# First pipeline step reordered: convolutions, pad clears, an integer-weight load and a gather change places

## The chip, the cores and the metric
One core of one Trainium2 chip. The metric is the device time of the kernel in microseconds (us), as a median of several executions.

## The reference
Sixteen images of 32 channels and 32 x 32 pixels go through a dense block and then through a quantised block. The dense block, cut to what matters:

```python
x1 = relu(conv2d(x, w1, b1, 2, 2))                       # 3x3, dilation 2
x2 = relu(conv2d(cat(x, x1), w2, b2, 2, 2))
x3 = relu(conv2d(cat(x, x1, x2), w3, b3, 2, 2))
x4 = relu(conv2d(cat(x, x1, x2, x3), w4, b4, 2, 2))
fea = einsum('ij,bcjk,lk->bcil', H, relu(cat(x, x1, x2, x3, x4)), H)
out = conv2d(fea, w6, b6, 1, 1) + x
```

The quantised block takes `out`, quantises activations and the weights w1, w2, w3 of its own to 4 bits (one scale for each whole tensor, from its largest magnitude), and computes a 1x1 convolution, a depthwise 3x3 convolution and a 1x1 convolution, with relu between them and a residual at the end.

## The kernel before
The images go in eight pairs; u = 0, 1 is the image in its pair. The dense block is a software pipeline of nine steps (`steps`): in step s each engine does the convolutions of pair s and the transform of pair s - 1. Step 0 has no transform to do, and its code has special cases under `is_first(s)`; step 8 has no convolutions. Every engine has its own instruction list, written out by hand, and engines wait for one another on semaphores. Nothing reorders the work of an engine.

Features 0 to 3 (x, x1, x2, x3) lie in SBUF as `D[f][u]`, 128 partitions: two quarters are the image's own rows, two are copies of them shifted by rows (halos), which the DMA makes out of the own rows (`halos(s, f, u)`: two transfers, lines 219 and 222; for f = 2 and u = 0 the second one is issued by ScalarE, `halo_2`, line 348). A high and a low part are kept of every feature for precision; `own_ready[u]` says that both stand. `clear_pads(f)` writes the zero borders of D[f] with eight small memsets on VectorE.

TensorE's work of a pair goes by weight groups:

- `conv0` or `conv0_first` (group 0, from x: sums of x1 and x2), `conv0_on` (group 1, from x: sums of x3 and x4), nine matmuls each. Neither needs a halo from the DMA: x is loaded with its shifted copies.
- `conv1_alone` (group 2, from D[1], six matmuls of the cross terms of x2), `conv1` (group 3, from D[1]), `conv2` (group 4, from D[2]), `conv3` (group 5, from D[3]). Each waits for the halos of its feature.

Around them: ScalarE's `relu` (x1, x3) and `take_part` (x2, x4) read the sums, `high_2` writes the high part of x2; VectorE's `split` and `split_2` write the parts of a feature and raise `own_ready`; `add_first` and `add_second` (together `add_parts`) join the halves of the sums of x2 and x4, and the second raises `added[u]`. `gather_x` and `gather(s, f, u)` on SyncE's queue copy the features into `F` for the transform (one transfer of line 229, two of line 239).

The weights of the quantised block (`w_int`) are loaded by SyncE's line 273 into `w_raw`, the buffer of the convolution weights, once the sixth of the low parts of these is made (`w_ready` at NM = 6). VectorE's `weight_peaks` (lines 594 to 596) finds their largest magnitudes, TensorE's `turn_peaks` transposes them (line 774), VectorE's `top_weights` reduces them, TensorE's `spread_weights` copies the result to all partitions (line 779), and step 1 needs the scales.

SyncE's list of step 0, and the wait that heads each transfer, sets when the halos go: two loads of x for the next pair, halos(1, 0), halos(1, 1), gather_x(0), gather(1, 0), gather_x(1), gather(1, 1), w_int, halos(2, 0), halos(2, 1), gather(2, 0), gather(2, 1), gather(3, 0), halos(3, 0), halos(3, 1), gather(3, 1), xb.

Of the kernel before, what the change touches and what calls it, by code (L numbers as in the profile page):

```python
# [77 lines left out]
def dense_block(nc, block, semaphore, x_res, x_pads, x_mix, w_conv, bias, w_mix, h_cols, h_rows, b6, w_int, ident_in, keep):  # L78
# [7 lines left out]
    with ExitStack() as ctx:  # L86
# [97 lines left out]
        def is_first(s):  # L184
            return isinstance(s, int) and s == 0
# [22 lines left out]
        @block.sync  # L208
        def _(sp):
            def load_x(s, p):  # L210
                for u in range(2):
                    sp.dma_start(x_own[p][u][:].rearrange("c a n -> c (a n)"),
                                 x_pads[s * 2 + u]).then_inc(x_in[p][u], 16)

            def halos(s, f, u):
                sp.wait_ge(own_ready[u], s * 3 + f)

                flat = D[f][u][:].bitcast(F32).rearrange("p h a n -> p h (a n)")
                sp.dma_start(flat[HALO_M2:HALO_M2 + 32, :, HALO:DSZ],
                             flat[OWN_T2:OWN_T2 + 32, :, 0:DSZ - HALO]).then_inc(halo_in[f][u], 16)  # L220
                if (f, u) != (2, 0):
                    sp.dma_start(flat[HALO_P4:HALO_P4 + 32, :, 0:DSZ - HALO],
                                 flat[OWN_T:OWN_T + 32, :, HALO:DSZ]).then_inc(halo_in[f][u], 16)

            def gather_x(s, u):

                if not is_first(s):
                    sp.wait_ge(f_lo[u], s)
                sp.dma_start(F[u][0:32].rearrange("p h n -> p (h n)"), x_mix[s * 2 + u]).then_inc(f0_in[u], 16)

            def gather(s, f, u):

                if f == 2:
                    sp.wait_ge(added[u], s * 2 + 1)
                else:
                    sp.wait_ge(relu_done[u], s * 2 + (f + 1) // 2)
                done, landed = (part[u], f2_in[u]) if f == 2 else (r[u], f_in[u])
                for h in range(2):
                    sp.dma_start(F[u][32 * f:32 * f + 32, h],
                                 done[32 * h:32 * h + 32].rearrange("p a b l -> p (a b l)")).then_inc(landed, 16)  # L240

            sp.dma_start(x_own[0][0][:].rearrange("c a n -> c (a n)"), x_pads[0]).then_inc(x_in[0][0], 16)
            sp.dma_start(w_raw[:, 0, :], w_conv[:, 0, :]).then_inc(w_in[0], 16)
            sp.dma_start(x_own[0][1][:].rearrange("c a n -> c (a n)"), x_pads[1]).then_inc(x_in[0][1], 16)
            sp.dma_start(bias_sb[:], bias).then_inc(c_in, 16)
            for n in range(1, NM):
                sp.dma_start(w_raw[:, n, :], w_conv[:, n, :]).then_inc(w_in[n], 16)
            sp.dma_start(hc[:].rearrange("p d l -> p (d l)"), h_cols).then_inc(h_in, 16)
            sp.dma_start(hr[:], h_rows).then_inc(h_in, 16)
            sp.dma_start(mix_raw.rearrange("p k m -> p (k m)"), w_mix).then_inc(mix_in, 16)  # L250
            sp.dma_start(b6_sb[:], b6).then_inc(c_in, 16)
            sp.dma_start(ident[:], ident_in).then_inc(id_in, 16)

            def step(s, odd, batch):
                p = s - 1
                if is_last(s):
                    return
                if not no_next(s):
                    if not is_first(s):
                        for u in range(2):  # L260
                            sp.wait_ge(x_split[u], s)
                    load_x(s + 1, 1 - odd)
                if is_first(s):
                    for u in range(2):
                        halos(s, 1, u)
                for u in range(2):
                    gather_x(s, u)
                    gather(s, 1, u)
                    if not is_first(s):
                        halos(s, 1, u)  # L270
                if is_first(s):
                    sp.wait_ge(w_ready, NM)
                    sp.dma_start(w_raw[:].rearrange("p n m -> p (n m)")[:, 0:W2], w_int).then_inc(int_in, 16)
                halos(s, 2, 0)
                halos(s, 2, 1)
                gather(s, 2, 0)
                gather(s, 2, 1)
                gather(s, 3, 0)
                halos(s, 3, 0)
                halos(s, 3, 1)  # L280
                gather(s, 3, 1)
                sp.wait_ge(mx_done, p + GRANT)
                sp.dma_start(xb[odd][:].rearrange("p u n -> p (u n)"), x_res[s]).then_inc(xb_in[odd], 16)

            steps(sp, step)
# [180 lines left out]
        def _(dve):  # L466
# [202 lines left out]
            def step(s, odd, batch):  # L669
                p = s - 1  # L670

                before = 1 - odd, batch - odd
                if is_last(s):
                    turn_s1(p - 1, 1)
                    turn_back(p - 1, 0)
                    turn_back(p - 1, 1)
                    add_up(p - 1, 0, *before)
                    turn_s1(p, 0)
                    add_up(p - 1, 1, *before)
                    turn_back(p, 0)  # L680
                    add_up(p, 0, odd, batch)
                    largest(p - 1, *before)
                    turn_s1(p, 1)
                    largest_last(0)
                    turn_back(p, 1)
                    add_up(p, 1, odd, batch)
                    largest_last(1)
                    return
                if is_first(s):
                    dve.wait_ge(zeroed, 2)  # L690
                if not is_second(s):
                    split(s, 1, 0)
                    if has_finish(s):
                        turn_s1(p - 1, 1)
                    split(s, 1, 1)
                if is_first(s):
                    for n in range(3, NM):
                        low_w(n)
                    low_mix()
                    clear_pads(2)  # L700
                add_parts(s, 2, 0)
                if is_first(s):
                    clear_pads(3)
                    dve.wait_ge(zeroed, 6)
                add_first(s, 2, 1)
                split_2(s, 0)
                add_second(s, 2, 1)
                split_2(s, 1)
                if has_finish(s):
                    turn_back(p - 1, 0)  # L710
                    turn_back(p - 1, 1)
                if not no_next(s):
                    low_x(s + 1, 1 - odd, 0)
                    low_x(s + 1, 1 - odd, 1)
                if has_finish(s):
                    add_up(p - 1, 0, *before)
                if is_first(s):
                    weight_peaks()
                if is_second(s):
                    quantise_weights()  # L720
                split(s, 3, 0)
                split(s, 3, 1)
                if is_first(s):
                    top_weights()
                if is_second(s):
                    sum_weights()
                    dve.wait_ge(fields_zeroed, 1)
                if has_finish(s):
                    add_up(p - 1, 1, *before)
                    largest(p - 1, *before)  # L730
                    into_fields(*before)
                if is_first(s):
                    low_f(s, 0)
                    split(1, 1, 0)
                add_parts(s, 4, 0)
                if is_first(s):
                    weight_scales()
                else:
                    low_f(s, 0)
                add_parts(s, 4, 1)  # L740
                low_4(s, 0)
                low_f(s, 1)
                if is_first(s):
                    split(1, 1, 1)
                else:
                    turn_s1(p, 0)
                low_4(s, 1)
# [4 lines left out]
        def _(pe):  # L752
# [55 lines left out]
            def conv0_on(s, u):  # L808
                weights(s, 2)
                conv(s, u, 0, 1, 1, True).then_inc(x_used[u], 1)  # L810
# [94 lines left out]
            def step(s, odd, batch):  # L905
# [28 lines left out]
                if is_first(s):  # L934
                    conv0_first(0)
                    conv0_first(1)
                    conv0_on(0, 0)
                    conv1_alone(0, 0)
                    conv0_on(0, 1)
                    conv1_alone(0, 1)  # L940
                else:
                    if is_second(s):
# [20 lines left out]
                conv2(s, 0)  # L963
                conv2(s, 1)
                if is_first(s):
                    turn_peaks()
                    conv0(1, 0)
                    conv0(1, 1)
                    spread_weights()
                if dct:  # L970
# [524 lines left out]
```

## Time and profile before

| | us |
|---|---|
| median of 3 runs | 396.76 |
| lowest of them | 396.33 |
| highest of them | 2032.51 |
| the profiled execution | 397.4 |
| its span, first to last instruction | 395.6 |
| its mean granted TensorE clock | 0.987 |

The median is the kernel's time here; one of the three runs was disturbed. The profile is of a further execution of 397.4 us, of which the span of 395.6 us is what the views show; 1.8 us lie around it. All times of rows are microseconds from the start of the span. Step 0 on TensorE ends at about 37.5 us.

### The profile page before, as it was taken

How to read it: one execution, taken by the hardware profiler on the slowest of the kernel's cores; microseconds unless marked ns; L12 is line 12 of the kernel's file. 1: busy time of each engine (PE TensorE's matmuls, PEld its weight loads, DVE VectorE, ACT ScalarE, POOL GpSimd, SP SyncE). 2: the span in 40 equal slices, each digit the busy share in tenths (PEclk: the TensorE clock that was granted, in tenths of full speed). 3: DMA queues.
4: the chain of work that ended last, by engine and by line, in shares of the span. 5: the costliest groups of instructions: out<-in, count | busy, mean ns of one | idle time of the engine just before them, and what ended most of it. 6: DMA issues, size and time to landing. Idle time of an engine off the chain costs nothing.

```text
span 395.6 us, 8022 instructions
## 1 busy us (share of the span) xinstructions
PE 372.0 (94%) x2873; PEld 270.7 (68%) x2873; DVE 289.1 (73%) x545; ACT 234.7 (59%) x377; POOL 13.5 (3%) x17
## 2 busy tenths in 40 slices
PE   8879999999999999899999999999984897999986
PEld 7657877888687878678786877887663443455532
DVE  5866678748937893696489378845986599677876
ACT  5436749545943864495468439544846696287761
POOL 6000000110030000000000000000000000000000
PEclk9999999999999999999999999999998699999999
DMA  7646336225333622463153334224200000000004
GB/s 235 193 134 181 86 92 167 67 54 124 109 93 75 170 54 54 102 159 83 44 124 111 79 80 118 59 54 103 64 2 0 2 0 0 2 2 3 2 27 186
DMA packets 19533, 32.56 MB, mean 82 GB/s; under 512 B 4528, under 2 KB 11568, under 8 KB 19504
## 3 DMA queue, kind: packets, MB, share of 16 engines
q1 hardware_dynamic: 18864, 31.14, 30.0%
q10 hardware_dynamic: 640, 1.03, 1.2%
q8 instruction: 18, 0.29, 0.3%
q14 instruction: 11, 0.09, 0.1%
HBM read 11.38 MB, written 2.10 MB: 34 GB/s over the span
## 4 chain that ended last, share of the span: by engine, by line
PE 78%; DVE 12%; DMA 4%; issue 3%; ACT 1%; DVEq 1%; ACTq 0%; SPq 0%
PE sums_ps L760 27%; PE mix_ps L863 12%; PE ps L1299 7%; PE mix_ps L892 5%; PE mix_ps L819 5%; PE sums_ps L819 5%; DMA D<-D 4%; PE mix_ps L867 4%; PE ps L1339 3%; PE ps L1266 2%; DVE part L493 2%; PE ps L1263 2%; PE mix_ps L901 1%; PE mix_ps L803 1%; DVE q_I L1182 1%
## 5 line engine op out<-in xcount | busy, mean ns | idle before, releaser
L760 PE MATMUL sums_ps<-D,w_hl 128*128 128x512 f32 x504 | 122.9, 399 | 2.2 <-DMA D<-D 2.2
L760 PEld LDWEIGHTS sums_ps<-D,w_hl 128*128 128x128 f32 x504 | 93.4, 188 | 32.5 <-issue 6.8
L863 PE MATMUL mix_ps<-mix_hl,F_hl 128*128 128x288 f32 x360 | 64.4, 296 | 0.2 <-ACT Y L384 0.2
L384 ACT ACTIVATE Y<-mix_ps 128x288 f32<-128x288 f32 x120 | 48.9, 410 | 24.8 <-PE mix_ps L867 12.9
L863 PEld LDWEIGHTS mix_ps<-mix_hl,F_hl 128*128 128x128 f32 x360 | 55.4, 190 | 2.5 <-ACT Y L384 0.8
L322 ACT ACTIVATE r<-sums_ps,bias_sb 64x512 f32<-64x512 f32 x28 | 19.1, 682 | 48.2 <-PE sums_ps L760 48.0
L493 DVE TENSOR_TENSOR part<-mix_ps,part 64x512 f32<-64x512 f32 x16 | 11.1, 694 | 41.0 <-PE mix_ps L819 40.6
L1065 ACT ACTIVATE q_I<-ps,w_bias 128x1024 f32 x24 | 25.4, 1110 | 16.6 <-PE ps L1299 16.6
L867 PE MATMUL mix_ps<-mix_hl,X 96*128 96x288 f32 x120 | 35.3, 298 | 0.0
L1299 PE MATMUL ps<-q_q,diag 64*64 64x512 bf16 x576 | 33.3, 388 | 0.4 <-DVE q_q L1160 0.4
L342 ACT ACTIVATE D<-part 64x512 fp32r<-64x512 f32 x16 | 10.7, 670 | 33.8 <-DVE part L499 33.8
L1299 PEld LDWEIGHTS ps<-q_q,diag 64*64 64x64 bf16 x576 | 19.2, 105 | 14.5 <-issue 0.9
L475 DVE CAST D<-r 64x512 fp32r<-64x512 f32 x32 | 13.4, 420 | 16.7 <-ACT r L322 16.1
L819 PE MATMUL sums_ps<-D,w_hl 128*128 128x512 f32 x96 | 24.0, 397 | 1.1 <-DMA D<-D 1.1
L892 PE MATMUL mix_ps<-Y,hc 32*32 32x512 f32 (+1 forms) x576 | 24.3, 567 | 0.6 <-ACT Y L384 0.6
L819 PE MATMUL mix_ps<-D,w_hl 128*128 128x512 f32 x96 | 23.8, 397 | 0.0
L558 DVE SCALAR_TENSOR_TENSOR values<-St,b_sb,xb 64x128 f32<-64x128 f32 (+1 forms) x64 | 22.2, 346 | 0.9
L477 DVE TENSOR_TENSOR D<-r,D 64x512 fp32r<-64x512 f32 x32 | 21.9, 685 | 1.1
L867 PEld LDWEIGHTS mix_ps<-mix_hl,X 96*128 96x128 f32 x120 | 22.4, 188 | 0.0
L525 DVE SCALAR_TENSOR_TENSOR X<-part,X 32x512 fp32r<-32x512 f32 x32 | 21.8, 680 | 0.7
L1266 PE MATMUL ps<-q_xq,w_q 128*128 128x386 bf16 x72 | 21.3, 362 | 0.0
L819 PEld LDWEIGHTS sums_ps<-D,w_hl 128*128 128x128 f32 x96 | 17.6, 189 | 5.2 <-DMA D<-D 1.6
(133 smaller groups left out, 513.6 us busy)
## 6 DMA issues: line engine op xcount, KB each, us to landing
D<-D SPq DMA_DIRECT2D x88, 126.0 KB, 2.3
x_own<-in_x_pads SPq DMA_DIRECT2D x16, 288.0 KB, 3.7
F<-r SPq DMA_DIRECT2D x64, 64.0 KB, 2.0
F<-in_x_mix SPq DMA_DIRECT2D x16, 128.0 KB, 2.4
F<-part SPq DMA_DIRECT2D x32, 64.0 KB, 2.0
xb<-in_x_res SPq DMA_DIRECT2D x8, 256.0 KB, 2.8
out<-q_res SPq DMA_DIRECT2D x8, 256.0 KB, 2.0
w_raw<-in_w_conv SPq DMA_DIRECT2D x6, 192.0 KB, 3.9
```

The costliest lines, as they stand in the source:

```text
L384: nc.scalar.activation(Y[:, u, g], banks(p, u)[:, g % 4, 0:MIX], ACT.Copy).then_inc(y_out, 1)
L477: nc.vector.tensor_tensor(out=own(f, u, 1), in0=src, in1=high.bitcast(F32), op=ALU.subtract).then_inc(own_ready[u], 1)
L525: last = nc.vector.scalar_tensor_tensor(out=X4[u][low, h], in0=part[u][k].rearrange("p a b l -> p (a b l)"), scalar=0.0, in1=X4[u][k, h].b ...
L558: last = nc.vector.scalar_tensor_tensor(out=keep.values[64 * pi:64 * pi + 64, batch, m, PH // 2 * a:PH // 2 * (a + 1), :], in0=st[k, pi], ...
L760: last = nc.tensor.matmul(conv_sums(s, u)[:, bank, :], w_hl[:, wp, n, d, :], D[f][u][:, xp, :, 4 * d:4 * d + RUN], start=start and d == 0 ...
L819: last = nc.tensor.matmul(side_sums(s, u, f), w_hl[:, w, n, d, :], D[f - 1][u][:, x, :, 4 * d:4 * d + RUN], start=d == 0 and w == 0, stop= ...
L863: nc.tensor.matmul(y, F_hl[u][:, xp, h, k], mix_hl[:, wp], start=n == 0, stop=False, skip_group_check=True)
L867: nc.tensor.matmul(banks(p, u)[:, g % 4, 0:MIX], X4[u][:, g // 4, NP * (g % 4):NP * (g % 4) + NP], mix4_hl[:], start=False, stop=True, ski ...
L892: last = nc.tensor.matmul(out[32 * dy:32 * dy + 32, j, 0:PX // 4 * len(us)], hc[k, d], y, start=d == 0, stop=d == 2, skip_group_check=True)
L1065: nc.scalar.activation(I[:, g, b, 0:PX], ps[:, 2 * b:2 * b + 2].rearrange("p k n -> p (k n)"), ACT.Relu, bias=keep.w2_bias[:, bass.ts(g, 1 ...
L1266: last = nc.tensor.matmul(c1_slot(ps, j)[:, h], w_q[:, bass.ts(k * 2 + par, NP)], x_low[:, at:at + CUT], start=j not in C1_OFFSET, stop=True)
L1299: last = nc.tensor.matmul(ps[64 * col:64 * col + 64, 2 * (two + b) + h], diag[rows, g, at:at + 2].rearrange("p q c -> p (q c)"), field[:, ...
```

## The change
Only step 0 is changed, and no instruction is added or taken away:

- TensorE does `conv0_on` of image 1 ahead of `conv1_alone` of image 0; and conv0 of the next pair's image 0 ahead of `turn_peaks`.
- SyncE issues the load of `w_int` right behind halos(1, u), ahead of the gathers; gather(2, 0) ahead of halos(2, 0); and halos(3, 0) ahead of gather(3, 0).
- VectorE does `clear_pads(3)` behind the `low_x` of the next pair, where `weight_peaks` stood, and `weight_peaks` between `split(s, 3, 0)` and `split(s, 3, 1)`.

```diff
@@ SyncE, step
                 if is_first(s):
                     for u in range(2):
                         halos(s, 1, u)
+                    sp.wait_ge(w_ready, NM)
+                    sp.dma_start(w_raw[:].rearrange("p n m -> p (n m)")[:, 0:W2], w_int).then_inc(int_in, 16)
                 for u in range(2):
                     gather_x(s, u)
                     gather(s, 1, u)
                     if not is_first(s):
                         halos(s, 1, u)
                 if is_first(s):
-                    sp.wait_ge(w_ready, NM)
-                    sp.dma_start(w_raw[:].rearrange("p n m -> p (n m)")[:, 0:W2], w_int).then_inc(int_in, 16)
+                    gather(s, 2, 0)
                 halos(s, 2, 0)
                 halos(s, 2, 1)
-                gather(s, 2, 0)
+                if not is_first(s):
+                    gather(s, 2, 0)
                 gather(s, 2, 1)
-                gather(s, 3, 0)
-                halos(s, 3, 0)
+                if is_first(s):
+                    halos(s, 3, 0)
+                    gather(s, 3, 0)
+                else:
+                    gather(s, 3, 0)
+                    halos(s, 3, 0)
@@ VectorE, step
                 add_parts(s, 2, 0)
                 if is_first(s):
-                    clear_pads(3)
-                    dve.wait_ge(zeroed, 6)
+                    dve.wait_ge(zeroed, 4)
                 add_first(s, 2, 1)
                 split_2(s, 0)
                 add_second(s, 2, 1)
@@ VectorE, step
                 if is_first(s):
-                    weight_peaks()
+                    clear_pads(3)
+                    dve.wait_ge(zeroed, 6)
                 if is_second(s):
                     quantise_weights()
                 split(s, 3, 0)
+                if is_first(s):
+                    weight_peaks()
                 split(s, 3, 1)
@@ TensorE, step
                     conv0_first(0)
                     conv0_first(1)
                     conv0_on(0, 0)
+                    conv0_on(0, 1)
                     conv1_alone(0, 0)
-                    conv0_on(0, 1)
                     conv1_alone(0, 1)
@@ TensorE, step
                 if is_first(s):
+                    conv0(1, 0)
                     turn_peaks()
-                    conv0(1, 0)
                     conv0(1, 1)
                     spread_weights()
```

## Rows read from the trace of the kernel before

**Rows 1.** The page, chain of work that ended last: shares by engine.
```profile
PE 78%; DVE 12%; DMA 4%; issue 3%; ACT 1%; DVEq 1%; ACTq 0%; SPq 0%
```

**Rows 2.** Timeline of TensorE, step 0: start us, us, what, [idle before, releaser].
```profile
9.97 2.25 PE L760 MATMUL mix_ps<-D,w_hl 128*128 128x512 f32 x9
13.36 1.65 PE L819 MATMUL sums_ps<-D,w_hl 128*128 128x512 f32 x6 [1.14 <-DMA D<-D]
14.85 2.25 PE L760 MATMUL mix_ps<-D,w_hl 128*128 128x512 f32 x9
16.94 1.56 PE L819 MATMUL sums_ps<-D,w_hl 128*128 128x512 f32 x6
18.34 4.36 PE L760 MATMUL mix_ps<-D,w_hl 128*128 128x512 f32 x18
23.38 2.36 PE L760 MATMUL mix_ps<-D,w_hl 128*128 128x512 f32 x9 [0.68 <-DMA D<-D]
27.68 2.39 PE L760 MATMUL mix_ps<-D,w_hl 128*128 128x512 f32 x9 [1.94 <-DMA D<-D]
...
29.93 4.43 PE L760 MATMUL sums_ps<-D,w_hl 128*128 128x512 f32 x18
```

**Rows 3.** Timeline of VectorE and ScalarE, 13 to 26 us, same columns.
```profile
13.30 0.34 DVE L649 TENSOR_TENSOR w_hl<-w_raw,w_hl 128x192 fp32r<-128x192 f32 x1
...
16.11 0.69 DVE L493 TENSOR_TENSOR part<-sums_ps,part 64x512 f32<-64x512 f32 x1
...
17.56 0.67 ACT L342 ACTIVATE D<-part 64x512 fp32r<-64x512 f32 x1 [3.94 <-DVE part L499]
...
18.73 0.18 DVE L641 MEMSET D<- 32x144 f32 x1
18.94 0.69 DVE L493 TENSOR_TENSOR part<-sums_ps,part 64x512 f32<-64x512 f32 x1
19.55 0.75 DVE L484 SCALAR_TENSOR_TENSOR D<-part,D 64x256 fp32r<-64x256 f32 x2
...
21.10 0.67 ACT L342 ACTIVATE D<-part 64x512 fp32r<-64x512 f32 x1 [2.87 <-DVE part L499]
...
21.80 0.75 DVE L484 SCALAR_TENSOR_TENSOR D<-part,D 64x256 fp32r<-64x256 f32 x2 [0.79 <-ACT D L342]
...
24.80 0.94 DVE L596 TENSOR_REDUCE stat<-w_raw 128x1 f32<-128x768 f32 x1
```

**Rows 4.** Timeline of SyncE's queue, 13 to 28 us: start, us of issuing.
```profile
13.32 0.58 SPq L229 DMA_DIRECT2D F<-in_x_mix  x1
13.95 1.20 SPq L239 DMA_DIRECT2D F<-r  x2
...
16.99 0.58 SPq L273 DMA_DIRECT2D w_raw<-in_w_int  x1
...
23.23 0.60 SPq L222 DMA_DIRECT2D D<-D  x1
23.88 4.21 SPq L239 DMA_DIRECT2D F<-part  x4
```

**Rows 5.** Line 348 (ScalarE's halo transfer), 20 to 21 us: issue to landing.
```profile
DMA to landing us min/median/max: 3.0/3.0/3.0
```

**Rows 6.** Line 222, the issue at 23.23 us alone: issue to landing.
```profile
DMA to landing us min/median/max: 4.4/4.4/4.4
```

**Rows 7.** The page, DMA issues: count, KB each, median us to landing.
```profile
D<-D SPq DMA_DIRECT2D x88, 126.0 KB, 2.3
```

**Rows 8.** DMA queues, 23 to 28 us: packets, MB, share of 16 engines.
```profile
q8 instruction: 1, 0.02, 2.2%
```

**Rows 9.** DMA issues, 14 to 32 us: count, KB each, median us to landing.
```profile
w_raw<-in_w_int SPq DMA_DIRECT2D x1, 843.0 KB, 4.8
```

**Rows 10.** Stages of 2 us: busy of each engine, clock, DMA share, GB/s.
```profile
310.00:312.00 2.00, 2.00 (x8) 0.93 (x7) 0.00 (x0) 1.61 (x2) 0.00 (x0) 0.50 0.04 8
...
314.00:316.00 2.00, 2.00 (x14) 0.97 (x11) 0.90 (x2) 1.97 (x4) 0.00 (x0) 1.00 0.00 0
```

## What I predict

> **What bounds it now.** I read the chain of work that ended last first: TensorE holds 78% of it [rows 1], so an edit in step 0 counts as far as it moves TensorE's list forward. Next TensorE's timeline of step 0. It has three holes, each ended by a halo transfer D<-D: 1.14 us ahead of conv1_alone(0) at 13.36, 0.68 ahead of conv2(0) at 23.38, 1.94 ahead of conv2(1) at 27.68 [rows 2]. Behind the last one TensorE runs on into the next pair's conv0 at 29.93 [rows 2]. So the start of conv2(1), 27.68, sets when step 0 ends, and the 1.14 us ahead of it matter only if the two later holes do not swallow them.
>
> What feeds these two? Backwards: the halos of x2 wait for split_2, that for add_parts, that for conv1_alone and for VectorE itself. VectorE starts add_first(0) at 16.11, 1.1 us after the sums of conv1_alone(0) end (13.36 + 1.65 = 15.01 [rows 2]), since it is in clear_pads(2) until then; and it has the eight memsets of clear_pads(3) ahead of add_first(1), which starts at 18.94, just behind the last memset [rows 3]. conv1_alone(1) had ended at 18.50 [rows 2]. The last view is SyncE's queue: the halo issued at 23.23 lands 4.4 us later, where the median of its kind is 2.3 [rows 4, 6, 7].
>
> **TensorE's swap.** conv0_on(1) moves into the hole. Nine matmuls take 2.09 us of TensorE's time (14.85 to 16.94) and six 1.40 to 1.49 [rows 2]. conv0_on(0) starts at 9.97 as now, conv0_on(1) at about 12.07, conv1_alone(0) at 14.16, conv1_alone(1) at 15.56, conv1 at 16.96 (now 18.34), done at 16.96 + 4.36 = 21.3. Both halos of x1 are there: the last was issued ahead of 13.32 [rows 4] and with 2.4 us lands by 15.1. conv1_alone(0) itself ends 0.8 us later than now, at 14.16 + 1.65 = 15.81. The cover is VectorE, busy in clear_pads(2) until just before 16.11 [rows 3]. Without it add_first(0) would be up to 0.8 us late. With it, it stays at 16.11.
>
> **VectorE without clear_pads(3) in front.** add_parts(0) ends at 17.52 as now (ScalarE's high_2 follows at 17.56 [rows 3]). conv1_alone(1) ends at 15.56 + 1.6 = 17.2, so add_first(1) runs 17.54 to 18.23, not from 18.94. split_2(0) waits for high_2 (17.56 + 0.67 = 18.23), runs 18.28 + 0.75 = 19.04; now its end is 20.30. That is 1.26 us earlier. From there the order is the old one: add_second(1) 0.68, high_2(1) 0.67, split_2(1) 0.75. Now this leads from 20.30 to 22.55, so it ends at 21.29 instead, 1.26 earlier.
>
> **SyncE's queue.** The queue is free at 13.3, but w_int waits for the sixth w_ready, 13.64 [rows 3, 4]. Behind this wait stand four gather groups, for which high_f waits, after 30 us: slack. Issues of 0.58 for w_int and each gather_x and 1.20 for each pair of gathers [rows 4]: w_int 13.67, gather_x(0) 14.28, gather(1, 0) 14.90, gather_x(1) 16.14, gather(1, 1) 16.76 to 17.90, and then gather(2, 0), whose data are there at 17.52: 17.94 to 19.16. halos(2, 0) is ready at 19.04. So this move costs 0.12 us on the path of one of its two transfers. The other is ScalarE's, unmoved behind its own wait, issued at 19.06; it takes 3.0 us [rows 5] and lands last, at 22.06. conv2(0) starts at about 22.1 instead of 23.38. The bounds for that transfer are 2.3 us [rows 7] and 3.0; I take 3.0, its own row. With 2.3, SyncE's would set it, at 19.18 + 2.3 = 21.5, and TensorE is busy until 21.3 anyway.
>
> SyncE's issues for image 1 follow split_2(1) at 21.3: lines 219 and 222, the second at 21.95 instead of 23.23. It still comes 0.15 us before the start of conv2(0). That matters for the 4.4 us. In that stretch one packet of an instruction queue holds one DMA engine for 2.2% of 16 x 5 us = 1.8 us [rows 8], and the halo lands 4.4 - 2.3 = 2.1 us late. SyncE is held too: four gather issues take 4.21 us where two take 1.20 [rows 4]. I take the fetch as TensorE's own, set off at a place in its list (its stretch, 23 to 28 us, is that of conv2(0), which starts at 23.38). Up to that place the same number of instructions stands in its list after the change, so it comes with conv2(0) again, and meets the halo again. conv2(1): 21.95 + 4.4 = 26.35, start 26.4, instead of 27.68: 1.28 us earlier. The bounds are a landing of 2.3 us (conv2(1) then starts when conv2(0) ends, 24.5) and one of 4.4. I take the upper one.
>
> The Trainium skill (Runtime: NRT & Kernel Launch, Instruction fetch mechanics) states that an engine's instructions come in 16 KiB blocks by its own DMA queue while it executes. By that rule the fetch is tied to the list and stays beside conv2(0), the sum above; with a fetch tied to clock time instead it would be the rival below. The 0.02 MB of the one packet agree with the block.
>
> A cost in the queue itself: w_int is 843 KB and lands 4.8 us after issue, where 126 KB take 2.3 [rows 7, 9]; that is 717 KB more in 2.5 us, 287 KB/us. It now passes in a lull. Put ahead, it lands at 13.67 + 4.8 = 18.5, and behind it stand gather_x and gather(1, u) of both images and gather(2, 0), 128 KB each by their shapes, 640 KB: 2.2 us more, until 20.7. Without w_int, gather(2, 0) would land at about 18.56 + 2.0 = 20.6. So the halos of 19.18 find the queue late by 0.1; the bounds are 0 and, at half that rate, 2.3 us. I take 0.1, since ScalarE's halo is issued now while w_int is still in flight (16.99 + 4.8 = 21.8 [rows 4, 9]) and takes only 3.0 us [rows 5].
>
> The Trainium skill (DMA: Bandwidth & Descriptors, Queues, rings and completion order) lets a DMA engine turn between queues packet by packet but keeps one queue's ring in order. By this rule the w_int load does stand in front of everything that SyncE issues later, and it speaks against the move; ScalarE's halo is spared. No row here shows this backlog.
>
> **What goes behind.** conv2(0) ends at 24.5, relu to 25.2, split(3, 0) to 26.4. clear_pads(3), 1.4 us, lies between low_x (ends about 22.8) and 25.2: free, with 1 us to spare. weight_peaks, three reductions of which the large ones take 0.94 each [rows 3], about 2.0 us, runs 26.4 to 28.4, while the relu of image 1 cannot be done before 26.4 + 2.39 + 0.7 = 29.5: free. turn_peaks now stands behind conv0(1, 0), at 31: its input is ready 2.5 us before, and top_weights follows by 31.9, ahead of spread_weights at 33.1. halos(3, 0) is issued at 26.4 instead of 29.39 and is needed at 33.3; it waited for nothing before, so no gain. halos(3, 1), 30.7 to 31.9, lands at 33.7, needed at 34.7. All of TensorE's later work shifts by what conv2(1) shifts.
>
> **Sum.** 1.28 earlier at conv2(1), less 0.1 for the queue: 1.2 us. The profiled execution, 397.4 with a span of 395.6, would give 396.2 and 394.4. The median shown is 0.64 below that execution: 396.76 - 1.2 = 395.5.
>
> **Rivals.**
> - *The fetch misses the halo.* It needs the fetch some 0.5 us later against line 222, or much earlier. For it: conv2(0) may start up to 0.6 us sooner if ScalarE's transfer lands like the others. Against: the two starts hang on the same chain. conv2(1) starts at 24.5, 3.2 us early; weight_peaks then holds split(3, 1) until 28.4, its halo lands at 32.5, when conv3(1) comes up: just hidden. 396.76 - 3.2 = 393.6. Chance 0.17.
> - *The gain is halved late.* At 310 us the granted clock is 0.50 (1.2 GHz), by 314 it is 1.00 (2.4 GHz), with TensorE busy in both [rows 10]. If the rise stays where it is in time, the 1.2 us of work drawn ahead of it run at half pace: gain 0.6, 396.2. Chance 0.13.
> - *Nothing is gained.* The holes only move: PE's earlier hole goes into the one before conv2(0), and the DMA queue's backlog takes VectorE's gain. 396.8. Chance 0.07.
> - *Slower: SyncE is held behind w_int.* One issue was held for some 1.8 us (4.21 - 2.40 [rows 4]). If that happens to a gather ahead of halos(2, 0), these go at 21.0, land at 23.5 with the next pair of transfers behind them, 0.2 to 0.5 us later than now: 397.1. It decides from a hold of 1.2 us up. Against it: w_int is in flight when halos are issued now, and those go at once. Chance 0.07.
>
> **Numbers.** The forecast has 0.56. The range goes from 393.4 (the missed fetch) to 397.0, which leaves out part of the first and of the last rival. What a measurement of this kernel can tell from no change is about 2%, 7.9 us. No case reaches that: 0.98 within it, 0.01 on either side.
>
> **What the profile after would show.** No hole ahead of conv1_alone(0) at 14.2; a hole of 0.7 to 0.9 us ahead of conv2(0), which starts at 22.0 to 22.3; conv2(1) at 26.3 to 26.6 with a landing of 4.4 for line 222 at about 21.95, and an instruction packet beside it; line 493's third run at 17.5 to 17.6; the next pair's conv0 at 28.6 to 28.9; no wait for line 779. A start of conv2(0) at 22.5 or later would show the backlog; a landing near 2.3 for line 222 would show that the fetch went elsewhere, and would be the first way for me to be wrong.

## The result, and the profile after

| | before | after |
|---|---|---|
| median us | 396.76 | 393.95 (9 runs, 392.94 to 396.07) |
| ratio, after to before | | 0.9936, 95% interval 0.9912 to 0.996 |
| profiled execution, us | 397.4 | 394.38 |
| its span, us | 395.6 | 392.6 |
| its mean granted clock | 0.987 | 0.986 |

The change gains 2.8 us, by the interval 1.6 to 3.5. I had forecast 1.2, as 395.5 us in a range of 393.4 to 397.0. The range holds the time, 0.55 us above its low end; the likeliest case does not describe it.

TensorE's timeline of the changed kernel, step 0, to be held against [rows 2] (start us, us, what, [idle before, releaser]; lines below the edits are numbered 6 to 8 higher):

```profile
9.90 4.37 PE L768 MATMUL mix_ps<-D,w_hl 128*128 128x512 f32 x18
14.10 2.96 PE L827 MATMUL sums_ps<-D,w_hl 128*128 128x512 f32 x12
16.90 4.37 PE L768 MATMUL mix_ps<-D,w_hl 128*128 128x512 f32 x18
22.88 4.46 PE L768 MATMUL mix_ps<-D,w_hl 128*128 128x512 f32 x18 [1.61 <-DMA D<-D]
27.18 2.25 PE L768 MATMUL sums_ps<-D,w_hl 128*128 128x512 f32 x9
29.27 0.27 PE L782 MATMUL sums_ps<-ident,stat 128*3 128x128 f32 x1
```

The hole ahead of conv1_alone is gone. The one ahead of conv2(0) has grown, from 0.68 to 1.61 us: conv2(0) starts at 22.88, not at 22.1 as summed. And the hole of 1.94 us ahead of conv2(1) has vanished: both conv2 stand in one group of 18 matmuls. The next pair's conv0 starts at 27.18 instead of 29.93, 2.75 us earlier.

VectorE and ScalarE, to be held against [rows 3]:

```profile
16.04 0.69 DVE L499 TENSOR_TENSOR part<-sums_ps,part 64x512 f32<-64x512 f32 x1
...
17.49 0.69 DVE L499 TENSOR_TENSOR part<-sums_ps,part 64x512 f32<-64x512 f32 x1
17.49 0.68 ACT L348 ACTIVATE D<-part 64x512 fp32r<-64x512 f32 x1 [3.94 <-DVE part L505]
18.20 0.75 DVE L490 SCALAR_TENSOR_TENSOR D<-part,D 64x256 fp32r<-64x256 f32 x2
...
20.45 0.75 DVE L490 SCALAR_TENSOR_TENSOR D<-part,D 64x256 fp32r<-64x256 f32 x2 [0.79 <-ACT D L348]
```

This part came as worked out. add_first(1) starts at 17.49, split_2 of the images ends at 18.95 and 21.20. Up to the halo transfers the 1.3 us are there.

SyncE's queue [rows 4], and then three landings of the changed kernel, each from its own line and issue: ScalarE's halo issued at 18.98, against [rows 5]; line 219 of 18.98, which took 2.5 in the kernel before; and line 222 of 21.89, against [rows 6]:

```profile
13.59 0.33 SPq L267 DMA_DIRECT2D w_raw<-in_w_int  x1
...
17.53 1.22 SPq L239 DMA_DIRECT2D F<-part  x2
18.98 2.87 SPq L219 DMA_DIRECT2D D<-D  x2
21.89 0.60 SPq L222 DMA_DIRECT2D D<-D  x1
```
```profile
DMA to landing us min/median/max: 3.9/3.9/3.9
```
```profile
DMA to landing us min/median/max: 2.9/2.9/2.9
```
```profile
DMA to landing us min/median/max: 2.3/2.3/2.3
```

ScalarE's halo of image 0 took 3.9 us where it took 3.0: this is the 0.8 us by which conv2(0) is late. The last halo took 2.3 us where it took 4.4: this is the hole that vanished. The DMA queues of the changed kernel from 24 to 26 us (packets, MB, share of 16 engines), against [rows 8]:

```profile
q8 instruction: 1, 0.02, 4.9%
```

The instruction packet is there, for 4.9% of 16 x 2 = 1.6 us. By the packet records it starts at 24.21; in the kernel before it starts at 24.67. The halo of 21.89 had landed at 24.2, just ahead of it. In the kernel before, the one of 23.23 would have landed at 25.5 and met it. So, against the sum that I had forecast, step 0 gained by being late: 0.8 us were lost ahead of conv2(0), and 2.1 us won behind it. This was luck, and it is step 0 alone; what it is worth in the whole time is taken up with the experiments.

### The profile page after: what moved, and what is told of

Same layout as the page of the kernel before. It is cut to its first block, busy times and chain, and to the rows that moved or that the text cites. A ratio compares the mean times of both kernels' runs of the same rounds, so it can differ in the third digit from the quotient of the medians.

```text
span 392.6 us, 8020 instructions
## 1 busy us (share of the span) xinstructions
PE 370.5 (94%) x2870; PEld 270.8 (69%) x2873; DVE 289.0 (74%) x545; ACT 234.6 (60%) x377; POOL 13.5 (3%) x17
## 3 DMA queue, kind: packets, MB, share of 16 engines
q10 hardware_dynamic: 640, 1.03, 1.2%
## 4 chain that ended last, share of the span: by engine, by line
PE 78%; DVE 11%; DMA 4%; issue 3%; ACT 2%; DVEq 0%; ACTq 0%
PE sums_ps L768 28%; PE mix_ps L871 12%; PE ps L1307 7%; PE mix_ps L900 5%; PE mix_ps L827 5%; PE sums_ps L827 5%; PE mix_ps L875 4%; DMA D<-D 4%; PE ps L1347 3%; PE ps L1274 2%; DVE part L499 2%; PE mix_ps L909 1%; PE ps L1271 1%; PE mix_ps L811 1%; DVE q_I L1190 1%
## 5 line engine op out<-in xcount | busy, mean ns | idle before, releaser
L768 PEld LDWEIGHTS sums_ps<-D,w_hl 128*128 128x128 f32 x504 | 93.5, 188 | 32.2 <-issue 6.3
L522 DVE SCALAR_TENSOR_TENSOR F_hl<-F,F_hl 128x1024 fp32r<-128x1024 f32 x16 | 19.5, 1217 | 2.1 <-ACT F_hl L364 1.8
```

The costliest lines, as they stand in the source:

```text
L768: last = nc.tensor.matmul(conv_sums(s, u)[:, bank, :], w_hl[:, wp, n, d, :], D[f][u][:, xp, :, 4 * d:4 * d + RUN], start=start and d == 0 ...
```

## The experiments

Places of step 0 in the profiled execution of each kernel, in us; "packet" is the start of TensorE's first instruction packet by the packet records, "hole" the idle time ahead of conv2(1):

| kernel | ScalarE halo, issue to landing | conv2(0) | packet | line 222 halo, issued, took | hole | next conv0 | ratio to before, interval |
|---|---|---|---|---|---|---|---|
| before | 3.0 | 23.38 | 24.67 | 23.23, 4.4 | 1.94 | 29.93 | |
| after | 3.9 | 22.88 | 24.21 | 21.89, 2.3 | none | 27.18 | 0.9936, 0.9912 to 0.996 |
| e1 | 3.0 | 22.68 | 26.22 | 22.57, 2.4 | none | 27.21 | 1.0065, 1.0025 to 1.0105 |
| e2 | 3.0 | 21.94 | 23.17 | 21.80, 4.0 | 1.54 | 28.04 | 0.9937, 0.991 to 0.9965 |
| e3 | 3.0 | 21.93 | 29.29 | 21.80, 2.3 | none | 26.37 | 1.0038, 1.0007 to 1.0068 |
| e4 | 3.9 | 23.34 | 19.83 | 22.35, 2.3 | none | 27.63 | 0.9988, 0.995 to 1.0025 |
| e5 | 3.0 | 23.60 | 24.82 | 23.46, 3.5 | see text | 29.52 | 0.9984, 0.9953 to 1.0016 |
| e6 | 3.0 | 26.11 | 27.32 | 26.00, 4.1 | 1.65 | 32.32 | 0.9987, 0.9964 to 1.001 |
| e7 | 3.0 | 22.20 | 23.43 | 22.07, 3.5 | 1.04 | 27.80 | 0.9913, 0.9881 to 0.9944 |
| e8 | 3.0 | 23.15 | 24.37 | 23.02, 3.5 | 1.03 | 28.78 | 0.9996, 0.9973 to 1.0019 |
| e9 | 3.0 | 25.69 | 29.20 | 25.59, 2.3 | none | 30.22 | 0.996, 0.9933 to 0.9988 |
| e10 | 4.1 | 23.43 | 25.81 | 22.18, 2.4 | none | 29.30 | 0.9925, 0.99 to 0.9949 |
| e11 | 3.0 | 22.52 | 24.43 | 21.77 by ScalarE, 3.1 | none | 27.13 | 0.9942, 0.9915 to 0.997 |
| e12 | 3.6 | 23.07 | 24.98 | 22.37, 2.3 | none | 27.38 | 0.9917, 0.9886 to 0.9947 |

Absolute places differ between executions, mostly for reasons outside the edits: conv0_on(0) starts at 9.97 in the kernel before and 9.90 in the changed one, at 9.8 in e2, e3 and e8, at 9.2 to 9.4 in e1, e6, e7, e9 and e11, and at 10.2 to 10.4 in e4, e5, e10 and e12. In e6 and e9 conv1_alone(0) then waited 3.40 and 2.96 us for its halo, and the granted clock was 0.50 from 16 to 18 us. So in these rows the distances between columns say more than the places.

**e1: TensorE's list made eight matmul records shorter ahead of step 0.** Four warm-up matmuls of 256 columns stand in for eight of 128; in the trace each shows as two records.

```diff
-            for _ in range(8):
-                nc.tensor.matmul(mix_ps[:, 3, 0:NP], ones[:], ones[:], start=True, stop=True)
+            for _ in range(4):
+                nc.tensor.matmul(mix_ps[:, 3, 0:2 * NP], ones[:], ones[:].unsqueeze(1).broadcast_to([NP, 2, NP]),
+                                 start=True, stop=True)
```

> The kernel before with four warm-up matmuls of 256 columns in place of eight of 128: eight matmul records fewer in TensorE's list ahead of step 0, nothing else. Theory L (the instruction packet comes at a place in TensorE's list, and its meeting with the halo costs 2.1 us): the packet comes in conv2(1) instead of conv2(0), about 1.2 us into it; line 222's halo of 23.2 lands in about 2.3 us instead of 4.4, conv2(1) starts at 25.7 instead of 27.7, the time falls by 1.9 us. Rival T (the packet comes by clock time or another engine's list): it stays at about 24.7, the landing stays 4.4 and the time is that of before.

In step 0 theory L was right: the packet came at 26.22, in conv2(1), the halo landed in 2.4, and the next conv0 started at 27.21, 2.7 us earlier than before. Of these, 0.7 were there at conv2(0) already; from conv2(0) to the next conv0 it is 4.53 us for 6.55, so the missed meeting is worth 2.0. But the kernel got slower, by the ratio 0.25 to 1.05% (1.0 to 4.2 us). TensorE in step 1 shows where the gain of step 0 went; first e1 (52 to 57 us), then its DMA queues from 52 to 54:

```profile
51.65 2.04 PE L760 MATMUL sums_ps<-D,w_hl 128*128 128x512 f32 x8
55.04 2.36 PE L760 MATMUL sums_ps<-D,w_hl 128*128 128x512 f32 x9 [1.35 <-DMA D<-D]
```
```profile
q8 instruction: 1, 0.02, 4.2%
```

A hole of 1.35 us stands ahead of conv2(1) of step 1, with the next instruction packet beside its halo. The kernel before has no such hole there. e1's waits from 40 to 130 us hold four for a halo (who waited for what: us in total, times, longest):

```profile
PE sums_ps L760 <- DMA D<-D: 2.9, 4, 1.4
```

One of them, 0.42 us at 51.31, the kernel before has too (0.40). The other three, 1.35, 0.53 and 0.63 us ahead of conv2(1) of steps 1 to 3, are new. Each has an instruction packet beside its halo. The eight records that the list is shorter move later packets too. These 2.5 us take back step 0's gain. They do not account for a kernel that is slower than before: the profiled execution of e1, the fastest of its ten, has a span of 395.4 us, 0.2 less than the kernel before. What the other nine lose beyond this no profile shows.

**e2 and e3: without the backlog.** The load of `w_int` is cut.

```diff
-sp.dma_start(w_raw[:].rearrange("p n m -> p (n m)")[:, 0:W2], w_int).then_inc(int_in, 16)
+sp.dma_start(w_raw[:].rearrange("p n m -> p (n m)")[:, WX:W2], w_int[:, WX:W2]).then_inc(int_in, 16)
```

> The changed kernel with w_int's load cut to its last 54 columns (27 KB of 843), so most integer weights are not loaded. Theory B (the backlog behind w_int delayed conv2(0) to 22.88 and thereby put the instruction packet behind the halo): without it conv2(0) starts at 22.1, the packet comes at 23.4 and meets line 222's halo again, which lands 4 us or more after issue; conv2(1) starts at about 26.3 instead of 25.1, and the kernel gets 1.2 us slower than the changed one although it moves less: about 1.3 us faster than before instead of 2.8. Rival N (w_int only delays, the packet has nothing to do with it): conv2(0) at 22.1, conv2(1) at 24.5, 0.6 us faster than the changed kernel.

The places are theory B's: ScalarE's halo in 3.0, conv2(0) at 21.94, the packet at 23.17, line 222's halo late again. TensorE of e2:

```profile
21.94 2.38 PE L768 MATMUL mix_ps<-D,w_hl 128*128 128x512 f32 x9 [0.73 <-DMA D<-D]
25.86 2.35 PE L768 MATMUL mix_ps<-D,w_hl 128*128 128x512 f32 x9 [1.54 <-DMA D<-D]
28.04 2.27 PE L768 MATMUL sums_ps<-D,w_hl 128*128 128x512 f32 x9
```

The kernel moves 0.8 MB less and its next conv0 starts 0.86 us later than the changed kernel's. The whole time, though, did not show the 1.2 us: its ratio to before is that of the changed kernel. The profiles show where the lead went: at the start of the first transform stage (line 892 before) e2 is 1.84 us ahead of the kernel before and the changed one 2.43; at the third 1.94 and 2.40; at the fourth, behind a hole near 160 us, 2.47 and 2.10. That hole, ahead of conv2(0) of step 4, is again one that a late halo ends, with a packet beside it: 0.60 us in e2, 1.42 in the changed kernel.

> The kernel of e2 (w_int's load cut to 27 KB, most integer weights not loaded) with the four wide warm-up matmuls of e1. Theory B with L: conv2(0) at 22.1, the packet comes in conv2(1), the halo lands in 2.3, conv2(1) starts at 24.5: 3.2 us faster than before, 0.5 faster than the changed kernel, 1.9 faster than e2. Rival N: no difference from e2.

Again step 0 as theory B with L has it (next conv0 at 26.37, the earliest of all), and again the rest of the list took it back: slower than before. TensorE has new holes of 1.83, 1.02 and 1.33 us ahead of conv2(1) of steps 1 to 3. One place missed: the packet was expected in conv2(1) and came at 29.29, behind it, with the same warm-ups as e1; why is not shown. "No difference from e2" and "1.9 faster than e2" were both wrong for the whole time.

**e4: the packet earlier.** Ten warm-up matmuls of 102 columns in place of eight of 128, in the changed kernel.

> The changed kernel with ten warm-up matmuls of 102 columns for eight of 128: four matmul records more in TensorE's list ahead of step 0. Theory L: the packet comes four matmuls earlier, 0.3 us into conv2(0), at about 23.2 instead of 24.2, and meets line 222's halo, issued at 21.9: it lands at 25.3 to 26 instead of 24.2, and conv2(1) starts 0.3 to 0.9 us late. Rival T: the packet stays at 24.2, no difference from the changed kernel.

Neither. The packet came at 19.83, 4.4 us earlier and not 1.0, in conv1 and ahead of the halo, which landed in 2.3. DMA queues of e4, 19 to 22 us:

```profile
q8 instruction: 1, 0.02, 2.8%
```

By its middle nearly the whole gain was lost, though (0.9988). Step 0 does not explain it: from conv2(0) to the next conv0 it takes 4.29 us for 4.30, and the longer warm-ups (4.59 us for 3.79) put this conv0 0.45 us later. In the profile a further part of the loss stands in steps 2 and 3: ScalarE's halo took 4.6 and 5.3 us with packets beside it, and TensorE waited 1.13 and 1.72 us ahead of conv2(0), where the changed kernel has no such wait. So a list longer by four records has later packets at halos too, as e1's shorter one has, but at others.

So the packet follows the place in the list, but TensorE's list is read ahead of the array. A place behind the wait of conv2(0) is reached only when the halo has landed; one just ahead of that wait is reached while conv1 still runs. I infer this from where the packets came; no run shows the reading itself. Rival T (clock time, another engine) is out.

**e5 to e8: the parts.** e5 is TensorE's first swap in the kernel before. e6 is VectorE's part, and `turn_peaks` behind conv0(1, 0) with it. e7 is e5 and e6 together, with SyncE's old order. e8 is SyncE's new order alone. Their edits are the blocks of the change's diff.

> The kernel before with TensorE's swap alone (conv0_on of image 1 ahead of conv1_alone of image 0). Theory V (VectorE's memsets are the next bound): no hole at 13.4, but add_first of image 1 still starts at 18.9 behind clear_pads(3), conv2(0) at 23.4, the instruction packet meets the halo, conv2(1) at 27.7: 0.0 us. Rival P (TensorE's hole counts by itself): 1.1 us faster.

Measured: no change (0.9984, with 1 in the interval). The interval does not rule out rival P's 1.1 us; the places do. The sums of conv1_alone(1) ended at 17.38, and add_first(1) started at 19.18, behind the memsets, as theory V has it, so conv2(0) started at 23.60, no earlier than before. In its profiled execution the granted clock was 0.57 and 0.58 in 24 to 26 and 26 to 28 us, behind a hole of 2.01 us ahead of conv2(0), and the 18 matmuls of conv2 took 6.05 us for 4.4; the hole ahead of conv2(1) can't be read there.

> The kernel before with clear_pads(3), weight_peaks and turn_peaks moved as in the change, but without TensorE's first swap and with the old queue order. Theory V: conv1_alone of image 1 ends at 18.5, so add_first of image 1 starts at 18.5 to 18.6 instead of 18.9, conv2(0) at 23.0, the packet meets the halo, conv2(1) at 27.3: 0.35 us faster. Rival: the pads alone bring the 1.3 us, as the memsets took 1.4.

No change either (0.9987), where 0.35 us can't be told from nothing; the rival's 1.3 us lie at the edge of the interval. From the end of conv1_alone(1) to the issue of ScalarE's halo it is 1.5 us, 1.8 in the kernel before: the 0.3 us of theory V, and not 1.3.

> Both of these together, with SyncE's old order (w_int issued at 17.0, no gather ahead of halos(2, 0)). Theory W (any 843 KB in flight when the halos go out at 19.0 delay them, wherever w_int stands): the halos land 0.6 to 0.9 us late, conv2(0) starts at 22.7 to 22.9, the packet comes at 24.1 and misses line 222's halo, conv2(1) at 25.1: 2.6 us of step 0 gained, as in the changed kernel. Rival Q (the new queue order makes the backlog): conv2(0) at 22.1, the packet meets the halo, conv2(1) at 26.4: 1.3 us gained.

0.9913. TensorE of e7:

```profile
22.20 2.38 PE L762 MATMUL mix_ps<-D,w_hl 128*128 128x512 f32 x9 [0.47 <-DMA D<-D]
25.61 2.35 PE L762 MATMUL mix_ps<-D,w_hl 128*128 128x512 f32 x9 [1.04 <-DMA D<-D]
27.80 2.27 PE L762 MATMUL sums_ps<-D,w_hl 128*128 128x512 f32 x9
```

Rival Q by the places: without the new queue order ScalarE's halo lands in 3.0 and the packet (23.43) meets the other one. In step 0 the gain is 2.1 us, more than Q's 1.3, as the halo landed in 3.5 us and not in 4.4. Swap and pads, each worth nothing measurable alone, bring all of the gain together: each hides behind the other. The changed kernel's next conv0 starts 0.6 us earlier than e7's, yet e7 is not slower, and the profiles show where. At the first transform stage e7 and the changed kernel are 2.09 and 2.43 us ahead of the kernel before, at the third 2.22 and 2.40, at the fourth 3.06 and 2.10. Between the last two stands conv2(0) of step 4; first the changed kernel, then e7:

```profile
159.88 4.47 PE L768 MATMUL sums_ps<-D,w_hl 128*128 128x512 f32 x18 [1.42 <-DMA D<-D]
```
```profile
158.94 4.46 PE L762 MATMUL sums_ps<-D,w_hl 128*128 128x512 f32 x18 [0.31 <-DMA D<-D]
```

The hole is 1.12 us in the kernel before, 1.42 and 1.44 in the two profiles of the changed kernel (the second is e12), and 0.31 and 0.37 in e7 and e10. There too a packet stands beside ScalarE's halo: the halo took 5.0 us in the changed kernel, 3.9 in e7.

> The kernel before with SyncE's new order alone. Halos of x2 go out at 20.3, when the load of w_int and the gathers behind it have drained: conv2(0) at 23.4, the packet meets the halo, conv2(1) at 27.7: 0.0 us. If the backlog reaches past 20.3, conv2(0) is late by up to 0.5 us, the packet comes later and may miss the halo, and step 0 ends up to 1.5 us earlier.

0.9996: the new queue order brings nothing that can be measured by itself (its interval leaves up to 1.1 us).

**e9 to e12: the shift of step 0 alone, another remedy, and a repeat.** e9 is e1 and e10 is e7, with the wide warm-ups and this behind `spread_weights()`, so that the lists of step 1 and later stand where they stood:

```diff
+            def make_up():
+                for _ in range(4):
+                    nc.tensor.matmul(sums_ps[0:32, 3, 0:1], ones[0:32, 0:32], ones[0:32, 0:1], start=True, stop=True)
```

> The kernel of e1 (kernel before, four wide warm-up matmuls for eight) with four tiny matmuls behind spread_weights, so that from step 1 on every instruction of TensorE's list stands where it stood in the kernel before, and only step 0 is shifted against the 16 KB blocks. Theory L2 (a list shifted by eight matmuls makes later instruction packets meet the halos of x2 in steps 1 to 4, which took back e1's gain): line 222's halo of step 0 lands in 2.3 to 2.4, conv2(1) starts by 25.1 to 25.7, no hole of 1 us ahead of a conv2 in steps 1 to 3, and the time falls by 2.0 to 2.6 us, 0.3 of it given up to the tiny matmuls. Rival: e1's loss has another cause (the warm-ups or the clock) and stays: slower than before by 0 to 2 us.

Theory L2 holds by the places: halo in 2.3, no hole ahead of conv2(1), and in 40 to 130 us TensorE waits for a halo once, 0.4 us, as in the kernel before, where e1 had 2.9 us. The packet came 3.5 us behind the start of conv2(0), as in e1. The same eight records cost 1.0065 without the make-up and give 0.996 with it. The gain is 0.5 to 2.7 us by the interval, with a middle of 1.6, under the 2.0 to 2.6 expected.

> The kernel of e7 (swap and pads, old queue order) with the same shift of step 0 alone. Theory L2: conv2(0) at 22.1, packet in conv2(1), halo in 2.3, conv2(1) at 24.5 instead of e7's 25.6; 1.1 us less the tiny matmuls' 0.3 faster than e7, 3.5 to 4.5 us faster than before. Rival: later steps eat it, as fast as e7.

0.9925, as e7 (0.9913) within the intervals, so by the time the rival held. In its profiled execution ScalarE's halo took 4.1: `w_int` had gone out at 17.23 and the halos at 19.27, 2.0 us behind it, where e7 has 2.8 us. TensorE waited 1.86 us ahead of conv2(0), and the clock fell to 0.55 from 24 to 26 us: the next conv0 started at 29.30. Theory L2's 24.5 for conv2(1) was not met, so this profile can't price the missed packet.

e11 lets ScalarE issue the second halo transfer of image 1 (`halo_2(s, 1)` behind `high_2(s, 1)`), and clears the pads ahead of `low_x`.

> The kernel of e7 with the second halo transfer of image 1's x2 issued by ScalarE beside SyncE's first one (as for image 0), and the pads of D[3] cleared ahead of low_x. The transfers go out 0.6 us earlier against the packet. Theory: most of them are through when the packet starts 1.25 us into conv2(0); conv2(1) starts at 24.5 to 25.0, 0.5 to 1.1 us faster than e7. Rival: ScalarE's own transfer takes 3.0 us where SyncE's takes 2.3, and the packet still meets it: conv2(1) at 25.6, no faster than e7.

The halo went out at 21.77 and took 3.1; conv2(1) followed with hardly a hole (18 matmuls in 4.77 us, for 4.46 without one). conv2(1) started at 24.95, as the theory had it. The step is faster (next conv0 27.13, e7 27.80, and both had started alike), the time is not: 0.9942.

> The changed kernel once more, beside the kernel before and the three above on one chip. ScalarE's halo of image 0 lands in 3.9 us again (backlog), the packet comes at about 1.3 us into conv2(0) and behind the halo of image 1, conv2(1) follows conv2(0) without a hole: 2.2 to 3.2 us faster than before. If the 22.9 of its profile was chance, conv2(0) starts at 22.1 and a hole of 1 us or more stands ahead of conv2(1).

0.9917, ScalarE's halo in 3.6, no hole ahead of conv2(1). The changed kernel's pattern was no chance. The packet came 1.9 us into conv2(0) here (and in e11), 1.3 in the first profile and 1.2 to 1.3 in the kernel before, e2 and e5 to e8, so this too varies.

## Why the prediction was right and wrong, point by point

- **What bounds it** held: TensorE's hole in front of conv1_alone is worth nothing alone (e5, 0.9984), and what moves conv2(1) moves step 0's end.
- **TensorE's swap and VectorE's memsets** held to 0.1 us: conv1_alone at 14.10 (14.16 foreseen), add_first(1) at 17.49 (17.54), halos ready at 18.95 (19.04), line 222 at 21.89 (21.95).
- **The queue's cost was mis-sized**: 0.1 us taken, 0.8 to 0.9 measured (3.9 us against 3.0; again 3.9 in e4 and 3.6 in e12, and 3.0 with `w_int` cut in e2 and e3). The backlog also stands in SyncE's own queue: the two gather_x behind `w_int` took 5.5 and 5.0 us to land, 2.6 and 2.5 in the kernel before. I priced the sum of the bytes at the mean rate of the load and looked at SyncE's transfer only. I said that ScalarE's halo, on its own queue, was unmoved; it was the one that came late. My reading that a turn between the queues spares it does not stand beside the 3.9 us. My bounds of 0 and 2.3 held it. The row that I leaned on, ScalarE's 3.0 with the load in flight, has 3.3 us between the two issues; e10, with 2.0, took 4.1. In e8, with the new order, the same transfer was issued at 20.11, 1.1 us later than in the changed kernel, and took 3.0: the backlog was over by then.
- **"Meets the halo again" was the step that failed.** I had placed the packet rightly, 1.3 us into conv2(0) and not at a clock time. But the halo's issue hangs on VectorE, and the packet on the landing of image 0's halo. A delay of this landing alone parts the two. The 0.8 us of the point above did this, and 2.1 us came free: the packet started 1.4 us behind the issue of line 222's halo in the kernel before, 2.3 in the changed one, just as the halo landed. It is the rival of the missed fetch, with 0.17, and its condition of 0.5 us later against line 222 was met, but by a way that I did not name: it needed conv2(0) late, and I looked for it early. That the time came near its 393.6 is luck: conv2(1) started at 25.1, not at 24.5, and e7, with the meeting, has as good a time. The Trainium skill (Runtime: NRT & Kernel Launch, Instruction fetch mechanics) has the blocks fetched by the engine's own queue during execution; the packets' places in e1, e4 and e9 agree, in so far as they move with the list.
- **The price of a meeting was taken as fixed.** The sum has 4.4 us, the one landing on record. Where a packet met line 222's halo again, it landed in 3.5 (e5, e7, e8), 4.0 (e2) and 4.1 us (e6). So with the meeting, too, 1.28 us was a low estimate: in e7 the next conv0 starts 2.1 us before that of the kernel before.
- **high_f was not slack.** high_f makes the high part of what was gathered in `F` (line 364, 358 before). Moving halos(3, 0) ahead of gather(3, 0) puts the gather behind a wait. ScalarE's timeline of the changed kernel:

```profile
28.08 0.69 ACT L342 ACTIVATE part<-mix_ps,bias_sb 64x512 f32<-64x512 f32 x1
31.28 1.06 ACT L364 ACTIVATE F_hl<-F 128x1024 fp32r<-128x1024 f32 x1 [2.52 <-issue]
```

  In the kernel before it started at 31.52, with no idle time. The gather of 28.55 and 29.2 lands 2.0 us later, at 31.2, and high_f follows. ScalarE then comes late to the transform: TensorE waits 0.51 us for it at 41.77, 0.16 before. So of 2.75 us 2.4 are left at the first transform stage. In e7, with the old order, high_f starts at 29.42 with no idle time, TensorE's wait is 0.16 us as in the kernel before, and its 2.1 us stay whole.
- **The rest of the kernel** keeps the shift between 2.1 and 3.0 us: 2.43 at the first transform stage, 2.10 at the fourth, 2.58 at the last of them, 3.0 at the end. The rival of the halved gain was wrong. The clock rose earlier, with the work. Stages of the changed kernel, against [rows 10] (the clock is the figure behind the five busy times):

```profile
308.00:310.00 2.00, 2.00 (x7) 0.89 (x6) 0.43 (x1) 1.09 (x2) 0.00 (x0) 0.50 0.00 0
310.00:312.00 2.00, 2.00 (x13) 1.12 (x12) 1.49 (x4) 1.41 (x2) 0.00 (x0) 0.94 0.01 4
```

  At 310 to 312 us the clock is 0.94, where the kernel before has 0.50, and the lead grows by 0.4 us from 309 to 322 us. In e12 the clock there is 0.66 and the lead falls by 0.1, so the added 0.4 is not shown to be the change's.
- **The chances**: no case reached 2%, and 0.98 stood there. The range held through its low end.

What stays open: e2 and e7 have the meeting of packet and halo in step 0 and are not measurably slower than the changed kernel, which has not. Their profiles give the larger hole at 160 us and high_f for it; one profile of each, and two of the changed kernel, don't tell how regular this is, nor why the halo there takes 5.0 us in one list and 3.9 in the other. That the missed packet is worth 1.7 to 2.0 us in step 0 is shown (e3 against e2, e1 against before). In the median only e9 prices it, at 0.5 to 2.7 us.

No version that beats the changed kernel beyond its interval was found. The swap with the late pads (e7) has all of the gain that can be measured; the queue's new order adds none.

## What to carry to other kernels

Two holes that hide each other have to be closed together; e5 and e6 alone would have been thrown away. Where a landing time stands out from its kind, look which packet of another queue ran beside it and what sets that one off: here a delay of 0.9 us of one transfer parted the two. A shorter or longer instruction list is an edit by itself: compare variants with equal lists, or make the count up.

## What the runs showed of the hardware that I had not expected

- An instruction packet of 16 KB holds a DMA engine for 1.0 to 1.8 us, and a halo beside it lands in 3.5 to 4.4 us instead of 2.3 (before, e2, e5, e6, e7, e8). The two go together: packets of 0.96 (e5, e8) and 1.18 us (e7) have halos of 3.5, those of 1.45 (e2), 1.57 (e6) and 1.78 us (before) have 4.0, 4.1 and 4.4.
- Four warm-up matmuls of 256 columns for eight of 128, the same number of columns in fewer instructions (3.71 us for 3.79), made the kernel 0.65% slower; four tiny matmuls took that back. The profile ties 2.5 us of it to packets beside halos from 52 to 126 us. Four records more, in e4, took the changed kernel from 0.9936 to 0.9988, 0.45 us of it by longer warm-ups.
- 843 KB on SyncE's queue, with 640 KB in eight gather transfers behind it, delayed a transfer on ScalarE's queue by 0.9 us, more than SyncE's own beside it (0.4, from 2.5 to 2.9); with the 843 KB cut to 27 (e2, e3) it took 3.0 again.
- A hole of 1.9 to 2.0 us ahead of conv2(0) was followed by a granted clock of 0.55 to 0.60 (between the levels of 1.2 and 2.4 GHz, as means over 2 us) in e5 and e10, and the same stretch ran at 1.00 in the others with holes of 0.3 to 1.6 us. The length of the hole does not settle it: the kernel before has 1.94 us ahead of conv2(1), behind 0.68 ahead of conv2(0), and runs at 1.00 from 28 to 34 us.
